# A pre-norm decoder layer: attention scores in split bf16 through DRAM, or in fp32 on quarters of the array's rows

## What is computed

```python
x = x + linear_attention(layernorm(x)) @ Wo.T + bo      # phi(q), phi(k) = elu + 1, causal
x = x + softmax_attention(layernorm(x), ctx)            # logits * 16**-0.5, no projection behind
x = x + ffn(layernorm(x))                               # ternary weights with a scale a row
# linear attention of a head: sum over t <= s of (q_s . k_t) v_t, divided by the sum of (q_s . k_t) + 1e-6
# ffn: h = silu(x @ w1.T * s1) * (x @ w2.T * s2);  h = gelu(h @ h1.T * sh1);  h = gelu(h @ h2.T * sh2);  out = h @ w3.T * s3
```

## Time and profile before

| | us |
|---|---|
| median of 3 runs | 1246.91 (1246.67 to 1248.2) |
| profiled execution | 1246.86 |
| its span, first to last instruction | 1245.0 |
| TensorE (PE) busy | 1138.8 |
| DVE, ACT, POOL busy | 655.4, 664.3, 409.1 |
| mean granted clock of TensorE | 0.97 of 2.4 GHz |

### The profile page before, as it was taken

One profiled execution on the slowest core, in us unless ns is written; L12 is line 12 of the kernel. 1 busy time (PEld: TensorE's weight loads), 2 busy tenths in 40 slices (PEclk: granted clock), 3 DMA queues, 4 the chain that ended last, 5 costly groups with the idle time before them and its releaser, 6 DMA issues.

```text
span 1245.0 us, 21774 instructions
## 1 busy us (share of the span) xinstructions
PE 1138.8 (91%) x7906; PEld 886.1 (71%) x7906; DVE 655.4 (53%) x1414; ACT 664.3 (53%) x1170; POOL 409.1 (33%) x440
## 2 busy tenths in 40 slices
PE   2755869999899999999999998999999999999997
PEld 2543656877678776777778776787778777787786
DVE  3434545545655666655655566455666556444411
ACT  2433435647556555747557564656557464545432
POOL 1542425332451416223351414424261323400300
PEclk8788889999999999999999999999999999999999
DMA  6358586873946567582856558384665739453642
GB/s 162 103 115 220 180 225 183 253 234 93 288 161 196 153 202 206 157 246 81 265 176 196 160 167 266 115 225 140 211 201 170 203 109 282 148 170 96 210 149 85
DMA packets 133212, 224.18 MB, mean 180 GB/s; under 512 B 15216, under 2 KB 79856, under 8 KB 133104
## 3 DMA queue, kind: packets, MB, share of 16 engines
q1 hardware_dynamic: 128560, 210.97, 57.3%
q10 hardware_dynamic: 4544, 11.80, 3.2%
HBM read 180.51 MB, written 53.48 MB: 188 GB/s over the span
## 4 chain that ended last, share of the span: by engine, by line
PE 75%; DMA 11%; DVE 4%; ACT 3%; SPq 2%; issue 2%; POOL 1%; ACTq 0%; POOLq 0%
PE bank L1002 38%; PE bank L846 8%; PE bank L882 7%; PE bank L866 6%; DMA rows_scratch<-qp 5%; PE bank L984 4%; DMA xqs<-rows_scratch 4%; PE bank L1017 3%; PE bank L874 2%; DMA weight_ring<-weights_scratch 2%; PE bank L934 2%; PE bank L855 2%; PE bank L838 1%; SPq L388 1%; POOL qp L491 1%
## 5 line engine op out<-in xcount | busy, mean ns | idle before, releaser
L1002 PE MATMUL bank<-hidden_a,weight_ring 128*128 128x512 f32 x1024 | 275.3, 408 | 0.5 <-ACT hidden_b L667 0.5
L1002 PE MATMUL bank<-hidden_b,weight_ring 128*128 128x512 f32 x1024 | 271.8, 404 | 0.0
L505 POOL TENSOR_TENSOR att_l<-att_l,cst 128x512 f32<-128x512 f32 x128 | 168.4, 1317 | 226.5 <-ACT att_l L598 226.5
L1002 PEld LDWEIGHTS bank<-hidden_a,weight_ring 128*128 128x128 f32 x1024 | 183.4, 188 | 40.8 <-issue 8.8
L1002 PEld LDWEIGHTS bank<-hidden_b,weight_ring 128*128 128x128 f32 x1024 | 182.3, 188 | 39.0 <-issue 7.9
L661 ACT ACTIVATE hidden_full<-bank,columns_sb 128x512 f32<-128x512 f32 x128 | 88.8, 694 | 111.8 <-PE bank L1002 111.2
L984 PE MATMUL bank<-hidden_b,weight_ring 128*128 128x512 f32 x512 | 136.7, 410 | 9.7 <-DVE hidden_full L800 8.1
L598 ACT ACTIVATE att_l<-bank 128x512 f32<-128x512 f32 x128 | 76.0, 598 | 94.8 <-PE bank L882 90.8
L984 PEld LDWEIGHTS bank<-hidden_b,weight_ring 128*128 128x128 f32 x512 | 94.6, 192 | 29.9 <-issue 10.5
L772 DVE TENSOR_REDUCE mx<-bank 128x4 f32<-128x512 f32 x128 | 84.7, 684 | 47.5 <-PE bank L882 46.7
L632 ACT ACTIVATE att_x<-bank 128x512 f32<-128x512 f32 x128 | 76.4, 598 | 58.5 <-PE bank L882 56.6
(11 more groups left out here) (105 smaller groups left out, 1886.6 us busy)
## 6 DMA issues: line engine op xcount, KB each, us to landing
weight_ring<-weights_scratch SPq DMA_DIRECT2D x160, 512.0 KB, 4.6
rows_scratch<-qp SPq DMA_DIRECT2D x32, 384.0 KB, 2.8
rows_scratch<-kp SPq DMA_DIRECT2D x32, 384.0 KB, 4.1
ks<-rows_scratch SPq DMA_DIRECT2D x64, 128.0 KB, 5.3
xks<-rows_scratch SPq DMA_DIRECT2D x64, 128.0 KB, 2.6
weights_scratch<-in_h ACTq DMA_DIRECT2D x16, 512.0 KB, 4.8
xn3T_scratch<-hidden_b SPq DMA_DIRECT2D x16, 512.0 KB, 5.2
weight_bits<-in_h SPq DMA_DIRECT2D x32, 256.0 KB, 4.3
```

The lines of the kernel that those rows point to most:

```text
L505: eng.tensor_tensor(slot, slot, causal.rearrange("p (o s) -> p o s", o=1).broadcast_to([P, 4, S]), ALU.mult)\
L1002: mm = eng.matmul(fb[n % 4][:, :], ring[:, slot, kk * P:(kk + 1) * P], src[:, part, kk, :], start=(kk == 0 and part == 0), stop=(kk == KH ...
```

## The change

It replaces the split scores by fp32 scores on quarters of the array's rows. For q, k, xq and xk there are no bf16 parts, no stores to and loads from DRAM. Heads lie in their natural order, two in each 32 partitions; the stationary (or, for `max`, the moving) operand is multiplied by a mask of the one head or the other: `kz` by two DVE products (step `k_heads`), `xkz` by two ACT copies with a scale for each partition, `xqf` by one. A score step now covers all 16 heads of a sequence: 16 fp32 matmuls of 32 rows x 128 by 32 rows x 128, four row quarters into four banks; a group has two `lin_scores`, two `max` and two `x_scores` steps. The shift is transposed four times (it stands in four column blocks) and enters `x_scores` as four bf16 matmuls of 2 rows by 512 columns. The readers (`lin_copy`, `max_of`, `x_exp`) still go bank by bank.

All eight banks are one pool. `lin_sums` and `x_sums` wait once for both of their score tiles and walk them in another order. In groups 0 to 3, `lin_sums` first issues eight matmuls that nobody reads, of another shape for each of the four pairs. `att_l` and `att_x` get four slots instead of three. Due times are new: FF0 84 instead of 112, group starts 0, 28, 66, 110, STRETCH 2.2; TURN stays 137. The planner puts off a step on TensorE if the banks it needs are not free by due times.

The diff, cut to its core:

```diff
-    FF0 = 112
+    FF0 = 84
-    EARLY = ((-0.02, 0.98), (31.83, 1), (62.07, 1.25), (106, 1.9))
-    STRETCH = 1.9
+    EARLY = ((0, 1.15), (28, 1), (66, 1.3), (110, 1.91))
+    STRETCH = 2.2
...
-            fb, pool = bank[0:4], bank[4:8]
...
+            while pending:
+                t, step, g, n = pending.pop()
+                if step in ("hidden", "w3"):
+                    uses = [n // 4] if n % 4 == 0 else []
+                elif step in ("lin_scores", "max", "x_scores"):
+                    uses = range(4 * n, 4 * n + 4)
+                else:
+                    uses = [n]
+                taken = sorted(range(8), key=lambda j: free_at[j])[0:len(uses)]
+                if uses and free_at[taken[-1]] > t:
...
-                def store_parts(name, g, parts):
...
-                def load_rows(name, g, b, rows, last):
...
-                def third(name, g, whole, parts):
...
+                eng.memset(nshift[:, :, :, :], 0.0).then_inc(const_ready, 1)
...
+                        for e in range(2):
+                            eng.activation(xkz[:, e, :, :], halves(pbank(step, g)), ACT.Copy, scale=head_mask[e]).then_inc(xk_done, 1)
...
-                        eng.dma_start(xqs[KR:KR + 2, n, :, :], shiftT[:, n, :]).then_inc(sh_rows[n], 16)
+                        eng.activation(shiftT[:, n, :], pbank(step, g, n)[:, 0:2 * S].bitcast(BF16), ACT.Copy).then_inc(sh_done, 1)
...
+                    elif step == "k_heads":
+                        eng.wait_ge(k_done, C * g + C)
+                        wait_count(eng, lin_s, GB * g)
+                        for e in range(2):
+                            eng.tensor_scalar(kz[:, e, :, :], kf[:, :, :], head_mask[e], None, ALU.mult).then_inc(kz_done, 1)
...
+                def unread(to, pair):
+
+                    for k in range(8):
+                        if pair == 0:
+                            eng.matmul(to[:, 32 * k:32 * k + 32], cst[:, k % 2 * 128:k % 2 * 128 + 128], ident[:, 0:32], start=True, stop=True)
+                        elif pair == 1:
+                            eng.matmul(to[:, 0:256], rounded[:, k % 2 * 128:k % 2 * 128 + 128], rounded[:, :], start=True, stop=True)
+                        elif pair == 2:
+                            eng.matmul(to[:, 0:128], rounded[:, k % 2 * 128:k % 2 * 128 + 128], rounded[:, 0:128], start=True, stop=True)
+                        else:
+                            eng.matmul(to[:, 16 * k:16 * k + 16], cst[:, k % 2 * 128:k % 2 * 128 + 128], ident[:, 0:16], start=True, stop=True)
...
+                    b = pair // 2
                     wait_pbank(eng, step, g, pair)
...
+                    if which == 0 and g < 4:
+                        unread(pbank(step, g, pair), pair)
+                    eng.wait_ge(ready, NU * g + 2 * pair + 2)
+                    for m in range(C):
+                        for n in (2 * pair, 2 * pair + 1):
+                            for e in range(2):
+                                j = 2 * (n % 2) + e
+                                mm = eng.matmul(pbank(step, g, pair)[32 * j:32 * j + 32, m * S:(m + 1) * S],
+                                                vt[:, b, 8 * m + 2 * (n % 4) + e, :], att[:, (NU * g + n) % slots, 2 * m + e, :],
+                                                start=True, stop=True, tile_position=(0, 32 * j))
...
-                    for j in range(4):
-                        mm = eng.matmul(pbank(step, g, n)[:, j * S:(j + 1) * S], stationary[0:rows, b, h + j, :],
-                                        moving[0:rows, b, h + j, :], start=True, stop=True)
+                    for r in range(4):
+                        wait_pbank(eng, step, g, 4 * b + r)
+                    if shifted:
+                        for r in range(4):
+                            eng.matmul(pbank(step, g, 4 * b + r)[:, :], onesb[32 * r:32 * r + 2, :], shiftT[32 * r:32 * r + 2, b, :],
+                                       start=True, stop=False, tile_position=(32 * r, 0))
+                    for m in range(C):
+                        for e in range(2):
+                            for r in range(4):
+                                j = 2 * m + e
+                                rows = slice(32 * r, 32 * r + 32)
+                                mm = eng.matmul(pbank(step, g, 4 * b + r)[:, j * S:(j + 1) * S], stationary(rows, e, m, b),
+                                                moving(rows, e, m, b), start=not shifted, stop=not shifted or j == 3, tile_position=(32 * r, 0))
...
-                                      nshift[:, n, :, :].rearrange("p a h -> p (a h)"), identb[:, :]).then_inc(sh_psum, 1)
+                        for j in range(4):
+                            mm = eng.transpose(pbank(step, g, n)[:, j * S // 2:(j + 1) * S // 2].bitcast(BF16), nshift[:, n, j, :], identb[:, :])
```

More of the change, by code:

```diff
@@ L101, in decoder_layer_program @@
         for b in range(GB):
[L102 to L110, removed]
+            u = 27.6 + 3.21 * b
+            steady("shift", b, vector=u - 0.34, tensor=u + 0.29, scalar=u + 0.9)
@@ L111, in decoder_layer_program @@
+            u = 34.4 + 7.19 * b
+            steady("x_turn", b, tensor=u - 0.09, vector=u - 0.4, gpsimd=u + 0.29)
+            steady("ln3", b, vector=u + 3.82)
+    exps = sorted(entry[0] for entry in engines["scalar"] if entry[1] in ("q", "k", "x_exp"))
     stretches = []
@@ L216, in decoder_layer_program @@
             ident, causal = cst[:, 0:128], cst[:, 128:256]
+            head_mask = [cst[:, 256 + e:257 + e] for e in range(2)]
             bq1, bk1 = (sb(n, [P, C]) for n in ("bq1", "bk1"))
@@ new lines, in decoder_layer_program @@
+            free_at, last_use, place, use_before = [-1e9] * 8, [None] * 8, {}, {}
+            pending, program["tensor"] = program["tensor"][::-1], []
+            while pending:
[8 more added lines that the diff above has]
+                if uses and free_at[taken[-1]] > t:
+                    t = free_at[taken[-1]]
+                    j = len(pending)
+                    while j > 0 and pending[j - 1][0] <= t:
+                        j -= 1
+                    pending.insert(j, (t, step, g, n))
+                    continue
+                program["tensor"].append((t, step, g, n))
+                for j, u in zip(taken, uses):
+                    place[step, g, u], use_before[step, g, u] = j, last_use[j]
+                    (engine, reader, m), _, _ = release(step, g, u)
+                    free_at[j], last_use[j] = nominal[engine][reader, g, m], (step, g, u)
@@ L650, in _ @@
                         wait_full(eng, g, n)
[L651 removed]
+                        eng.activation(full[:, n % NFULL, :], pbank("gate", g, 2 * n)[:, :], ACT.Tanh, scale=s1h[:, n:n + 1]).then_inc(gate_tanh, 1)
                     elif step == "gate_round":
@@ L660, in _ @@
                         wait_full(eng, g, KH + n)
-                        eng.activation(full[:, (KH + n) % NFULL, :], fb[n % 4][:, :], ACT.Gelu, scale=sc).then_inc(h_full, 1)
+                        eng.activation(full[:, (KH + n) % NFULL, :], pbank("hidden", g, n)[:, :], ACT.Gelu, scale=sc).then_inc(h_full, 1)
                         if n == 0:
@@ L1025, in _ @@
                 wait_freed(eng, *last_use[0])
-                eng.matmul(pool[0][0:1, 0:1], low[:, NWB * 8:NWB * 8 + 1], causal[:, P - 1:P], start=True, stop=True).then_inc(low_psum, 1)
+                eng.matmul(bank[0][0:1, 0:1], low[:, NWB * 8:NWB * 8 + 1], causal[:, P - 1:P], start=True, stop=True).then_inc(low_psum, 1)
         ctx = ExitStack()
```

413 lines of the change are left out of this document (151 added, 262 removed).

## The result

The changed kernel takes 1201.8 us (median of 4 runs, 1199.95 to 1204.85) against 1247.56 for the kernel before beside it: ratio 0.9635, 95% interval 0.9612 to 0.9658. Forecast were 1214 us and 1188 to 1265. The profiled execution took 1201.23 us, its span (first to last instruction) is 1199.4.

The account below looks back on a forecast made before the run. TensorE was taken to bound full turns, the chain of the first two groups the ramp. 1245.0 - 39.0 to the first turn's end + 3 + 6.4 - 3 for the clock = 1212.4 span, so 1214 us; range 1188 to 1265.

Parts of the forecast that it names:

- A score step costs 1.02 us: New fp32 score step on TensorE: 32 instructions at the linear sums' 27 ns plus 0.16 us; 12.2 us a turn.
- two rivals with slow quarters: Score steps: weights not hidden in a quarter (1292 us, chance 0.12), or no concurrency of row quarters (1450 us, chance 0.07).
- the first rival: Score steps: a quarter's next weights wait for its matmul, 1.88 us a step, +10.4 us a turn, 1292 us; chance 0.12.
- The full turn: Full feed-forward turns on a full TensorE: +3.6 us of additions, -1.8 fewer pieces, -0.8 waits; net +1.0 us a turn.
- fewer pieces: Feed-forward matmuls in a full turn: up to 36 breaks by score steps go, half counted, -1.8 us a turn.
- The ramp: Before the first gate: missing DRAM round trips save about 26 us a group in groups 0 and 1; gate from 167.5 to 115.5.
- The two places in group 0: Ramp: linear scores start near 20.2 to 20.5 us, 10.8 saved; xq copy to max scores keeps 0.60 us, 12.6 saved.
- The 52 us for two groups' trips: Ramp: about 26 us saved in each of groups 0 and 1, the two savings adding up ahead of the first gate.
- The first turn: First feed-forward turn: 151.7 - 7.4 xqs wait + 13 work moved in - 3 group 4 + 10.4 unread matmuls = 164.7 us.
- The end: After the first turn: +3 us for group 4, 6.4 turns at +1.0 us, and -3 us for the clock.
- The clock: TensorE's granted clock in the ramp: with gaps filled, some of the time at 1.2 GHz returns, -3 us.
- Banks: Rival: with eight shared PSUM banks, scores or feed-forward wait for ACT's or DVE's reads, 2 to 7 us a turn; chance 0.16.

Follow-up runs that it names:

- quarter_by_quarter: Changed kernel with all eight instructions of one row quarter in a score step issued before the next quarter's: 1392.62 us, ratio 1.1142 to the kernel before.
- traffic_free: Changed kernel plus the old stores and row loads in all 16 groups, two row buffers, only SP waiting for them: 1219.82 us, ratio 0.9741.
- ring_late: Changed kernel with the weight ring's due times on SP put back 5.6 us later, as before the change: 1198.6 us, ratio 0.9575.
- late_ramp_trips: late_ramp with the DRAM round trips of trips_g01 in groups 0 and 1: 1281.26 us, ratio 1.0245 to the kernel before.
- trips_g01: Changed kernel with DRAM round trips of the old sizes put back in groups 0 and 1, first score steps waiting for them: 1280.95 us, ratio 1.0233.
- late_ramp: Changed kernel with wider due times in the ramp only (FF0 112, group starts 0, 36, 90, 138): 1224.05 us, ratio 0.9791 to the kernel before.
- unread_g01: Changed kernel with the unread matmuls in groups 0 and 1 only, instead of 0 to 3: 1193.42 us, ratio 0.9543 to the kernel before.

## Why the prediction was right, step by step

**A score step costs 1.02 us: right, but for 0.1 us ahead of it.** From start to next start it is 0.99 (515.91 to 516.90), and over five full turns 12.8 us a turn against the forecast 12.2. The column quarters of the linear sums were the right row to go by, though the weights are four times as wide. What that reading leaves out stands in front of the step: the last full-array matmul before a step on quarters takes 0.095 us longer to the next start (0.325 against 0.231 for a feed-forward matmul; 0.149 against 0.056 for an old score matmul ahead of linear sums). With it a step costs 12.83 / 12 + 0.095 = 1.16 us. Of the two rivals with slow quarters, quarter_by_quarter refutes one (a quarter's own weights wait: 0.111 us an instruction was measured, not 0.215) and shows the condition of the other: without neighbours from other quarters it is 2.75 us a step and 1393 us in all. The rule that stood beside the first rival, from the Trainium skill, TensorE: Matmul & The Clock Gate, Part 3 (The mechanism), does not hold for these fp32 rows: the load of a quarter's next weights, 187 ns long, starts within a few ns of that quarter's matmul, and the next matmul 0.111 us later.

**The full turn: sign wrong, +1.0 us forecast, -1.5 measured.** Taken from the starts of successive matmuls over five turns, us a turn, before and after. A gap counts to the matmul ahead of it:

| | before | after | forecast of the difference |
|---|---|---|---|
| score steps | 11.36 | 12.83 | +1.9 |
| shift in x_scores | 0 | 0.90 | +1.0 |
| shift transposes | 0.43 | 0.82 | +0.7 |
| feed-forward matmuls | 92.03 | 90.36 | -1.8 (fewer breaks), -0.8 (waits) |
| linear and x sums | 9.22 | 8.36 | none |
| projections, other transposes | 30.15 | 28.50 | none |

As the table stands, the additions come to 2.8 of the forecast 3.6. But the 0.095 us ahead of each of the 12 score steps a turn lie in the feed-forward row, and ten of those ahead of the linear sums lie in the score row of before. Put where they belong, scores went from 10.4 to 14.0 us a turn, and the additions are 4.8: the sum had them 1.2 too low. The step that failed is "fewer pieces": the feed-forward matmuls lie in 53 pieces a turn, before in 52, since other steps took the places of the score steps. Its -1.8 did not come. What came instead are waits that went, where the sum had 0.8: in the five full turns TensorE waited 8.1 us for DVE at the gates, 5.6 for the ring and 4.5 at score steps and shift transposes before, and 2.9 in all (2.5 of it for `ctxs`) after, so 3.1 us a turn less. The linear and x sums, which now wait once for two tiles, lie in 10 pieces a turn instead of 16. The 1.65 us of the last row were not taken apart. So the net of +1.0 lay near -1.5 by misses that partly cancelled. What took the feed-forward waits away is not settled. traffic_free excludes the lighter DMA by itself, ring_late the earlier ring loads by themselves; both edits together were not tried. For the gate's waits for DVE the pool of eight banks is left, and DVE's smaller load (83.9 us in the turn of the earlier trace rows, 75.5 in the one that answers to it), both argued only.

**The ramp: right in kind.** The two places in group 0 were forecast to the tenth (20.2 to 20.5 against 20.52; 0.60 against 0.65). The 52 us for two groups' trips were not measured: adding trips cost 57 us in late_ramp_trips and 78 in trips_g01, but trips whose row loads take SP twice as long as the old ones. What the traces do show is that of the 38 us of idle time that went ahead of the first gate, 31 were waits at score steps (34.8 before, 4.2 after). The first gate came 12 us later than the forecast 115.5. 6.6 of that are the unread matmuls of groups 0 to 2, which I had at nothing in the ramp; group 2's fell there, not into the first turn, and of the 15.6 us of all three only 9 hid. The rest, some 5 us, was not taken apart. What the forecast lacked is a term for the order: the same waits in a wide order come 24 us later (late_ramp). Whether trips in the chain make a wide order necessary is open, and the runs speak against it: with the slow trips the tight order ended no later than the wide one. The kernel before with a tight ramp was not tried, so how much of the 40.1 us new due times alone would have given is not known.

**The first turn: 164.7 forecast, 151.9 measured.** In its steps: -7.4 for the xqs wait. The work moved in: up to the first gate, before and after, instructions of the q projection, eight a step:

```profile
L846 PE MATMUL bank<-xn1T,wq 128*128 128x256 f32 x32 | 9.5, 450 | 0.8 <-ACT xn1T L562 0.8
```

```profile
L768 PE MATMUL bank<-xn1T,wq 128*128 128x256 f32 x24 | 7.6, 474 | 1.5 <-ACT xn1T L510 1.5
```

Counted so for all projections, five fewer steps of 1.73 us were done by then: +8.7 instead of +13. At the end of the turn three fewer: -5.2 instead of -3. Unread matmuls of group 3 alone: +4.2 instead of +10.4. 151.7 - 7.4 + 8.7 - 5.2 + 4.2 = 152.0. That this meets 151.9 so well is partly luck: it has neither the additions of the full turn (4.8) nor the turn's other waits (3.7 us before, 0.6 after). The misses of ramp (+12) and turn (-13) are of one kind, and at the end of the first turn, 279.3 us against the forecast 280.2, they had cancelled.

**The end.** Behind it the sum had +3 + 6.4 - 3 = +6.4 us, measured was -5.7: five turns of -1.5, then +3.5 in the seventh, and -1.8 in the last. The seventh has 23 more projection instructions than before (56 against 33), three steps of 1.73 us: it pays for the steps that were late. These 12.1 us are nearly the whole distance from 1212.4 to 1199.4.

**The clock: a term that was perhaps too small.** Half clock ahead of the first gate fell by 41 us and was put at 3 us of gain. No run edits the clock alone, but executions of one kernel differ in it. Over 28 of the kernel before (mean clock 0.961 to 0.972, 1246.64 to 1260.1 us) the time rises by some 0.4 us for each us more at half clock (worked out from mean clock and span); in unread_g01 it is 10 us for 26, also 0.4. Time and clock go together there; that the clock is the cause is not shown, since a wait lengthens the one and can lower the other. By that ratio, an estimate, 41 us are worth up to some 16 us, not 3. It can't be added to the trips' 52: a matmul of the chain at half clock is in both. The unread matmuls held the clock for 7 us, 3 us by the same estimate, and still lost. **Banks:** the waits that this rival needed did not come; TensorE waited 0.6 us for a reader at the gates in the whole span.

## What to carry to other kernels

Where small products leave most rows of the array empty, put four of them on row quarters, with one from each quarter next to each other in the list: the same instructions cost 1.0 us in that order and 2.75 us quarter by quarter. Count some 0.1 us for each change from the full array to quarters, too. A round trip through DRAM that a full engine hides in steady state is paid in the ramp; the order of the ramp has a price of its own there, 20 to 24 us here. When a removed step is put back to price it, compare its own rows with the old ones first: these trips came back twice as slow. Matmuls that nobody reads are to be tried against their absence: here they kept the clock for some 7 us and cost 12.

## What was not expected of the hardware

A bf16 matmul of 512 columns on two rows costs nothing beside three others like it (0.23 us for four). Weight loads of 128 fp32 columns into four row quarters start within 10 ns of each other and all lie in a round of 111 ns, as short as that of one quarter alone. The step from the full array to quarters costs 0.095 us, whether rows or columns are quartered (after a feed-forward matmul 0.325 instead of 0.231 us). And going from a DMA share of 0.36 to 0.64 in full turns left TensorE's turns as they were; the 16.5 us that the same loads cost in the ramp lay mostly in SP's queue, behind a wait.
